# Expert stage of a gated cross-attention block: first layer two tiles ahead, weight copies and row transposes three ahead, rings of four

## What is computed

```
x = x + tanh(g_xattn) * attention(layernorm(x), ctx, ctx)
z = layernorm(x)
logits = z @ gate;  top 2 of 8, softmax over the two gives the weights
expert n:  y = (silu(z @ w0[n]) * (z @ w1[n])) @ wo[n]
x = x + tanh(g_ffn) * sum over the two chosen experts of weight * y
```

## Time and profile before

| | us |
|---|---|
| timed runs, median of 3 | 551.46 |
| timed runs, lowest and highest | 549.7 and 552.86 |
| the profiled execution: span from its first to its last instruction | 665.6 |
| the same: PE busy with matmuls | 561.5 |
| the same: ACT busy | 431.8 |
| the same: DVE busy | 393.9 |
| the same: POOL busy | 384.0 |

### The profile page before, as it was taken

The page is one execution under the profiler, slowest core; times in us unless marked ns, Lnnn a source line. Parts: engine busy times, 40 slices in busy tenths (PEclk is TensorE's granted clock), DMA queues, the critical chain, the costliest instruction groups (busy, mean ns, idle before and its releaser), DMA issues.

```text
span 665.6 us, 21070 instructions
## 1 busy us (share of the span) xinstructions
PE 561.5 (84%) x6123; PEld 468.0 (70%) x6124; DVE 393.9 (59%) x1418; ACT 431.8 (65%) x1090; POOL 384.0 (58%) x524
## 2 busy tenths in 40 slices
PE   8998898998989899899898779787778978888960
PEld 6886676776767677677776668676677868877860
DVE  6797787777778677677778643372133323223663
ACT  4897787887787788788777735344244546556540
POOL 3347756576575666657566466575545555545651
PEclk9999999999999999999999899897899999999995
DMA  3801111111111111111112112233222222225996
GB/s 91 240 20 57 42 42 52 36 55 40 48 44 36 56 40 48 48 33 58 41 55 63 33 50 73 64 98 101 85 64 80 77 74 76 76 68 174 270 272 206
DMA packets 64242, 52.98 MB, mean 80 GB/s; under 512 B 8607, under 2 KB 60064, under 8 KB 64176
## 3 DMA queue, kind: packets, MB, share of 16 engines
q1 hardware_dynamic: 46560, 30.79, 16.5%
q0 software_dynamic: 8448, 16.93, 7.7%
q10 hardware_dynamic: 9168, 4.46, 2.3%
HBM read 29.44 MB, written 23.22 MB: 79 GB/s over the span
## 4 chain that ended last, share of the span: by engine, by line
PE 51%; another core or an unknown queue 15%; issue 10%; ACT 8%; DVE 6%; ACTq 3%; DMA 2%; DVEq 2%; POOL 1%; SPq 1%; POOLq 0%
PE psK L583 10%; PE psH L603 8%; PE psH L483 5%; PE psH L489 4%; PE psG L498 4%; PE psH L498 3%; PE psK L471 3%; ACT wcur L757 3%; PE psO L619 2%; ACTq L319 2%; ACT ys L771 2%; PE psK L619 2%; ACT hs L764 2%; PE psO L518 2%
## 5 line engine op out<-in xcount | busy, mean ns | idle before, releaser
L1251 POOL DMA_INDIRECT results<-ys,zin x136 | 136.1, 1001 | 106.5 <-ACT ys L771 68.3
L603 PE MATMUL psH<-zT,wcur 128*128 128x128 f32 (+1 forms) x760 | 139.1, 333 | 20.1 <-ACT wcur L757 15.2
L1178 POOL DMA_INDIRECT lists<-zp,dest x128 | 129.6, 1012 | 34.8 <-issue 31.1
L603 PEld LDWEIGHTS psH<-zT,wcur 128*128 128x128 f32 x760 | 112.8, 195 | 34.4 <-ACT wcur L757 20.1
L1083 DVE TENSOR_TENSOR hm<-psH,hs 128x512 f32<-128x512 f32 x68 | 47.0, 692 | 121.0 <-remote 45.7
L977 DVE TENSOR_REDUCE mx<-psH 128x8 fp32r<-128x512 f32 x128 | 82.5, 686 | 43.4 <-PE psH L483 23.6
L696 ACT ACTIVATE ex<-psH,rs 128x512 f32<-128x512 f32 x128 | 86.8, 688 | 23.9 <-PE psH L489 16.3
L583 PEld LDWEIGHTS psK<-v,pT 128*64 128x64 f32 x2048 | 69.6, 137 | 37.1 <-issue 36.3
L583 PE MATMUL psK<-v,pT 128*64 128x64 f32 x2048 | 81.1, 226 | 9.0 <-issue 8.6
L757 ACT COPY wcur<-w 128x512 f32 x95 | 56.1, 619 | 15.2 <-issue 14.2
L747 ACT COPY v<-kvr 64x64 f32<-64x64 f32 x256 | 63.7, 249 | 2.2
(11 more groups left out here) (176 smaller groups left out, 1140.5 us busy)
## 6 DMA issues: line engine op xcount, KB each, us to landing
yy<-results SPq DMA_DIRECT2D x16, 512.0 KB
zin<-lists SPq DMA_DIRECT2D x41, 130.0 KB
out_dram<-x ACTq DMA_DIRECT2D x16, 256.0 KB
xring<-in_x_dram SPq DMA_DIRECT2D x31, 128.0 KB
cring<-in_ctx_dram SPq DMA_DIRECT2D x31, 128.0 KB
zin<-lists SPq DMA_DIRECT2D x54, 65.0 KB
results<-ys,zin POOLq DMA_INDIRECT x136
w<-in_L_ffn_w_kernel_dram SPq DMA_DIRECT2D x2, 1024.0 KB, 7.1
```

Of the source, the lines that this page charges most:

```text
L603: last = pe.matmul(bank[t.buf(2)][:, k * ET + c.start:k * ET + c.stop], wcur[:, t.buf(2), h, a, k * P:(k + 1) * P], zT[:, t.buf(2), c], st ...
L1178: nc.gpsimd.indirect_dma_start(lists, bass.IndirectOffsetOnAxis(ap=dest[:, t.buf(4), j:j + 1], axis=0), zp[:, t.buf(4), j, :], None).then_ ...
L1251: nc.gpsimd.indirect_dma_start(results, bass.IndirectOffsetOnAxis(ap=zin[:, t.buf(8), h, D:D + 1].bitcast(U32), axis=0), ys[:, t.buf(8), h ...
```

## The change

The pipeline of the expert stage gets one step more ahead (`ahead=3`). In step s, PE now does the row transposes of s+3, the first layer of s+2 and the second layer of s; ACT the weight copy of s+3, the silu of s+2, the output of s; DVE the copy of s+3 and the product of s+2. `hm` becomes a ring of four. `wcur` has the same four halves as before, but an early tile uses one half (ring of four), a late tile two of them (ring of two) by the new function `wslot`. `zT`, `hs`, the PSUM banks, `zin` and `ys` keep their rings; SP and POOL are not touched.

```diff
-EXPERTS = Pipeline(NET, behind=1, ahead=2, unroll=8, steady=18, turns=2)
+EXPERTS = Pipeline(NET, behind=1, ahead=3, unroll=8, steady=18, turns=2)
...
-        wcur = sb("wcur", [P, 2, 2, 2, HID])
+        wcur = sb("wcur", [P, 4, 2, HID])
...
-        hm = sb("hm", [P, 2, 2, ET])
+        hm = sb("hm", [P, 4, 2, ET])
...
+        def wslot(t, h):
+
+            return 2 * t.buf(2) + h if late(t) else t.buf(4)
...
                 def rows_turned(s):
-                    if t := EXPERTS.at(s, 2):
+                    if t := EXPERTS.at(s, 3):
...
                 def first_products(s):
-                    if t := EXPERTS.at(s, 1):
+                    if t := EXPERTS.at(s, 2):
...
                 pe.wait_ge(on_done, NT)
+                rows_turned((None, 0))
+                first_products((None, 0))
                 second_layer((None, 0))
...
                 def weights(s):
+                    if t := EXPERTS.at(s, 3):
+                        e = [expert(act, t, h) for h in range(2 if late(t) else 1)]
+                        wait_for(act, b_ps, t, back=2 if late(t) else 4)
...
-                    if t := EXPERTS.at(s, 1):
+                    if t := EXPERTS.at(s, 2):
                         wait_for(act, a_ps, t)
...
+                weights((None, -3))
+                attention_step((None, NT + 1))
                 weights((None, -2))
-                attention_step((None, NT + 1))
+                attention_step((None, NT + 2))
                 weights((None, -1))
-                attention_step((None, NT + 2))
                 nc.scalar.activation(warm[:, :], tg[:, 0:1], ACT.Silu).then_inc(warm_done, 1)
+                silu((None, -2))
                 silu((None, -1))
                 weights((None, 0))
                 silu((None, 0))
...
                 def products(s):
-                    if t := EXPERTS.at(s, 1):
+                    if t := EXPERTS.at(s, 2):
...
-                        wait_for(dve, y_ps, t, back=2)
+                        wait_for(dve, y_ps, t, back=4)
```

More of the change, by code:

```diff
@@ L571, in attention_step @@
                         pe.wait_ge(place_done, NT - 4)
-                        rows_turned((None, -2))
-                        first_products((None, -1))
+                        rows_turned((None, -3))
+                        first_products((None, -2))
                     if t := ATT_PE.at(s, 2):
@@ L603, in first_products @@
                                     last = pe.matmul(bank[t.buf(2)][:, k * ET + c.start:k * ET + c.stop],
-                                                     wcur[:, t.buf(2), h, a, k * P:(k + 1) * P],
+                                                     wcur[:, wslot(t, h), a, k * P:(k + 1) * P],
                                                      zT[:, t.buf(2), c], start=True, stop=True)
@@ L618, in second_layer @@
                             for k in range(2):
-                                last = pe.matmul(psY[t.buf(2)][:, h * D:(h + 1) * D], hm[:, t.buf(2), k, h * P:(h + 1) * P],
+                                last = pe.matmul(psY[t.buf(2)][:, h * D:(h + 1) * D], hm[:, t.buf(4), k, h * P:(h + 1) * P],
                                                  wo[:, bass.ds(e[h], 1), k, :].squeeze(1), start=(k == 0), stop=(k == 1))
@@ L658, in _ @@
                 ATT_PE.run(pe, attention_step, since=ATT_PE.first + 2, until=NT - 3)
+                rows_turned((None, -2))
+                attention_step((None, NT - 2))
                 rows_turned((None, -1))
-                attention_step((None, NT - 2))
-                rows_turned((None, 0))
                 for n in (exp_done[0], exp_done[1], p_sb[0], p_sb[1]):
                     pe.wait_ge(n, NT)
-                first_products((None, 0))
+                first_products((None, -1))
                 attention_step((None, NT - 1))
@@ L752, in weights @@
                 def weights(s):
-                    if t := EXPERTS.at(s, 2):
+                    if t := EXPERTS.at(s, 3):
                         e = [expert(act, t, h) for h in range(2 if late(t) else 1)]
-                        wait_for(act, b_ps, t, back=2)
+                        wait_for(act, b_ps, t, back=2 if late(t) else 4)
                         for h, n in enumerate(e):
-                            last = nc.scalar.copy(wcur[:, t.buf(2), h, :, :], w01[:, bass.ds(n, 1), :, :].squeeze(1))
+                            last = nc.scalar.copy(wcur[:, wslot(t, h), :, :], w01[:, bass.ds(n, 1), :, :].squeeze(1))
                         last.then_inc(w_done, 1)
                 def silu(s):
-                    if t := EXPERTS.at(s, 1):
+                    if t := EXPERTS.at(s, 2):
                         wait_for(act, a_ps, t)
@@ L779, in experts_step @@
                 def experts_step(s):
-                    if static(s, NFULL - 2):
+                    if static(s, NFULL - 3):
                         act.wait_ge(late_table, LATE_READY)
@@ L989, in attention_step @@
                     if static(s, NT - 2):
-                        inputs((None, -1))
+                        inputs((None, -2))
                     if (t := ATT_DVE.at(s, 4)) and t.buf(2):
@@ L1044, in attention_step @@
                     if static(s, NT - 3):
-                        inputs((None, -2))
+                        inputs((None, -3))
                     if (t := ATT_DVE.at(s, -2)) and t.buf(4) == 3:
@@ L1111, in _ @@
                 attention_step((None, NT - 2))
-                inputs((None, 0))
-                products((None, -1))
+                inputs((None, -1))
+                products((None, -2))
                 attention_step((None, NT - 1))
                 attention_step((None, NT))
+                products((None, -1))
+                inputs((None, 0))
                 products((None, 0))
```

2 lines of the change are left out of this document (1 added, 1 removed).

## The result

The changed kernel takes 555.72 us (median of 6 runs, 554.16 to 557.59) against 550.89 us before (6 runs): ratio 1.0088, 95% interval 1.0066 to 1.011. It is slower by 0.9%, some 4.8 us (3.6 to 6.1).

What follows compares the result with a forecast made beforehand. It took the timed expert stage as nearly all TensorE work, with the profile's waits mostly that run's own. Start 0.40, end 1.67 and row loads 1.3 sum to +3.4 us on 551.46: 554.8 us, range 547 to 559.

Steps and rivals of the forecast that it cites:

- The two paces: Whole kernel: the profiled run slows down (attention tiles 4.79, then 5.92 us apart), while timed runs keep the early pace.
- rival "faster": Expert stage: the profile's 20.9 us of waits for hm are in the timed runs too; 547.6 us, chance 0.17.
- what could be won at most, 3 to 9 us: Expert stage, timed runs: nearly all TensorE work, so better overlap can win at most 3 to 9 us.
- Steady state, nothing: Expert stage between start and end: instruction counts stay equal on TensorE; gain between 0 and 8.9 us, taken as 0.
- Start, +0.4: Start of expert stage: third weight copy ahead of the first silu lengthens ScalarE's chain; +0.40 us, bounds 0 and 0.61.
- first reader of P(t): Steady state: between a tile's first layer and the reader of its hm product lie another 1.10 us of TensorE work.
- End, +1.67: Behind the last first layer: POOL has one tile more of scatters to do; +1.67 us, bounds 0 and 2.56.
- Row loads, +1.3 (0 to 2.6): Tiles from 60 on: row loads behind fetches lose one step of margin before the row transposes; +1.3 us, 0 to 2.6.
- It never set the pace: Late row loads before the change: their round had four steps, at most 2.74 us each, so it was not limiting.
- The middle of the stage: Tiles 8 to 28: POOL's eight list scatters (10.2 us) may delay row transposes by at most 0.89 us; taken as 0.
- early on it is wide: Row loads of early tiles: wide margin, needing only an output copy two steps (5.66 us) before the row transposes.

## Why the prediction was right or wrong

*The two paces* held. A second profile spans 548.1 us, its attention tiles are 4.86 us apart, its expert stage waits 0.6 us for hm. The rival "faster" was a reading of the first profiled execution, and so was what the Trainium skill's rule on repeated gaps ("Perfetto Trace Analysis", Optimization Strategy) would make of it: at the timed pace the gaps were not there. The size of what could be won at most, 3 to 9 us, was about right: F(1) to F(67) takes 197.1 us in the second profile, and 40 steps of 2.84 and 26 of 2.90 would take 189.0. But only 0.6 of these 8.1 us were waits for hm.

*Steady state, nothing*: right. F(30) to F(58) takes 80.49 us in both kernels.

*Start, +0.4*: the mechanism was right, the size was not; 0.9 us were lost. The term counted the copy's 0.61 us but not the register read in front of it (0.36 us), which until then had lain under a wait. And it is F(2), with S(0) 1.04 us later, that waits: F(2) fills the bank that P(0) reads. (So the prediction's "first reader of P(t)" is, after the change, F(t+2).)

*End, +1.67*: without the crowd 1.68 was measured, by the predicted mechanism. In the kernel as it is it came to 2.2 in the pair of profiles: the two scatters more are 1.34 and 1.33 us apart instead of 1.28, and G(65) starts 532.99 - 528.07 = 4.92 us after the last F began, where before G(66) did so after 4.43. Before, POOL ran back to back from G(65) on, so that G(66) waited for POOL; after, G(65) waits for its outputs. A slow register read ahead of Y(65) (0.75 us) may be part of that, which was not tested.

*Row loads, +1.3 (0 to 2.6)*: the place was right, the size too small by the pair of profiles: 2.6 us; all profiles together leave 0.6 to 2.7. The margin of T alone, a step shorter, costs 3.1 (28.68 to 31.75 us). "It never set the pace", said of the rows before the change, holds: no T waits for rows there. What the term had wrong is that late rows are all that the crowd of fetches costs. Against the 25.87 us without fetches the late tiles lose 2.8 us before, with no wait for rows at all, and 5.4 after, of which such waits are 2.2; with T behind F, where they are 0.2, 4.8 are still lost. The register reads, which the prediction did not have, are slow in both kernels. And T waited at tiles 63 and 64, not at 64 to 67.

The middle of the stage, set to 0 with 0.89 as its bound, came to 0.6; "early on it is wide" overlooked that POOL lags 9.3 us there.

By the pair of profiles the sum came to 554.8 because three terms were small by about 0.5, 0.5 and 1.3 us and one was left at 0 that cost 0.6. The pair gives +6.2, the timed runs +4.8 (3.6 to 6.1); the prediction gave +3.4. That 554.8 lies within 1 us of the measured 555.72 is in part luck: the three runs that it started from stood 0.57 us above the median of all six.

## What to carry to other kernels

Before pricing a wait, see whether the profiled execution ran at the timed pace: the same work early and late in one trace, and span against median, told here that 20.9 us of waits were not there to win. A longer lead shortens the margin of whatever feeds the first stage and lengthens the drain behind the last; look for the engine or queue that already lags there (POOL by 9.3 us) and shorten its lag first: that gave 0.5%, where the lead cost 0.9%.

## What was not expected of the hardware

- One execution of the same program was profiled at 665.6 us and another at 548.1; only the slower one had the late hand-overs from TensorE. What slowed it is open.
- Register reads from a table in SBUF take up to 1.15 us (median 0.31 on TensorE, 0.49 on ScalarE) while the DMA engines are 91% busy, and at most 0.45 us (0.30 and 0.29) at 24%; a page of busy times does not show them, the listing of the source line does.
- In two profiled executions the first F of the stage took 3.46 and 3.56 us instead of 1.96, without a wait of its own. The granted clock is what differs. The windows from 323.40 to 325.00 us (the clock stands before the DMA share), the run with Y caught up at step 44 first, then the changed kernel:

```profile
323.40:325.00 1.60, 1.60 (x4) 1.33 (x5) 0.27 (x4) 0.77 (x2) 0.66 (x1) 0.50 0.30 89
```

```profile
323.40:325.00 1.60, 1.60 (x11) 1.14 (x11) 0.00 (x0) 0.36 (x1) 1.07 (x1) 1.00 0.33 88
```

So TensorE ran at the lower of its two levels (1.2 instead of 2.4 GHz), and the other execution shows the same 0.50 from 323.60 to 326.60 us. From 320 to 323 us TensorE had been busy for 1.75 us there and 1.69 in the other execution, but for 1.66 in the changed kernel, whose clock stayed at 1.00. Why it fell in these two is open.
